# Keys and values given a place for the whole kernel, their rows fetched in the front's last steps, and edges counted in groups of two columns

## What is computed

```python
deg = maximum(segment_sum(ones, dst), 1)
h = relu(layernorm(x))
hw = norm * (h @ weight)                     # norm = deg ** -0.5
x = x + relu(segment_sum(hw[src], dst) * norm + bias)
x1 = relu(layernorm(x)); y = x1
for l in range(2):
    q, k, v = y @ Wq.T + bq, y @ Wk.T, y @ Wv.T
    scores = einsum(q[dst], k[src]) / 8      # softmax over the edges of one dst
    attn = segment_sum(softmax(scores) * v[src], dst) @ Wo.T + bo
    y = batchnorm(y + attn); y = batchnorm(y + ff(y))
x = x + layernorm(y)
```

## Time and profile before

| | |
|---|---|
| median of three runs | 3460.18 us |
| the profiled execution, its own time | 3465.55 us |
| its span, first to last instruction | 3463.7 us |
| PE, DVE, ACT, POOL busy | 3034.8, 2354.1, 1951.4, 2176.8 us |
| granted TensorE clock, mean | 0.960 |
| front's second part, first to last tile started | 359.5 to 936.8 us |
| attention of layer 0 begins | 991.2 us |

### The profile page before, as it was taken

How to read it: one execution, slowest core, us unless ns; L and a number is a source line. 1 busy time by engine, 2 the same in 40 slices (tenths; PEclk the granted TensorE clock), 3 DMA queues, 4 the chain that set the end, 5 groups by cost and what they waited for, 6 DMA issues and landing times. The chain is left out here.

```text
span 3463.7 us, 72225 instructions
## 1 busy us (share of the span) xinstructions
PE 3034.8 (88%) x24802; PEld 2390.4 (69%) x24802; DVE 2354.1 (68%) x6951; ACT 1951.4 (56%) x3918; POOL 2176.8 (63%) x1979
## 2 busy tenths in 40 slices
PE   2360899999947999999999989989999999999985
PEld 2120466666636888888888877767888888888875
DVE  9798344343426888888888854218888888888856
ACT  0120444444426777787877731227777787777734
POOL 2788888888006777777777720007777777777734
PEclk9995999999978999999999999999999999999987
DMA  9544776666379999998999841239999999999951
GB/s 371 81 82 94 148 133 118 125 121 123 97 171 167 166 166 166 175 167 166 168 165 168 154 98 24 48 73 171 165 165 166 169 173 165 164 164 171 153 121 59
DMA packets 1294527, 497.26 MB, mean 144 GB/s; under 512 B 1236806, under 2 KB 1262431, under 8 KB 1285974
## 3 DMA queue, kind: packets, MB, share of 16 engines
q1 hardware_dynamic: 1153262, 460.73, 67.5%
q0 software_dynamic: 133120, 0.80, 4.1%
q10 hardware_dynamic: 7788, 31.21, 2.7%
HBM read 154.06 MB, written 80.99 MB: 68 GB/s over the span
## 5 line engine op out<-in xcount | busy, mean ns | idle before, releaser
L1377 DVE CUSTOM_DVE_ANT_0 prob<-s_ps,mask 125x500 f32<-125x500 f32 x1600 | 1058.3, 673 | 307.6 <-PE s_ps L1224 231.1
L1146 POOL TENSOR_TENSOR staged<-prob,staged 125x500 f16<-125x500 f32 x960 | 1064.5, 1115 | 155.1 <-ACT staged L1140 85.8
L1314 ACT ACTIVATE prob<-prob,neg_max 125x1000 f32<-125x1000 f32 (+1 forms) x960 | 954.7, 994 | 120.7 <-DVE scrap L1383 118.3
L1224 PE MATMUL s_ps<-keys,queries 128*125 128x500 f16 x3200 | 947.2, 378 | 43.0 <-DMA values<-v_heads 25.4
L444 POOL DMA_INDIRECT counts<-count,cell x320 | 678.6, 2121 | 182.9 <-issue 106.8
L1255 PEld LDWEIGHTS o_ps<-values,across 125*125 125x125 f16 x7680 | 592.4, 139 | 223.1 <-issue 49.9
L1255 PE MATMUL o_ps<-values,across 125*125 125x128 f16 x7680 | 608.0, 222 | 60.6 <-DMA across<-staged 60.1
L1140 POOL CAST staged<-prob 125x500 f16<-125x500 f32 x640 | 385.5, 602 | 419.4 <-ACT prob L1314 259.1
L1390 DVE TENSOR_TENSOR p_lo<-t_ps,p_hi 125x500 f16<-125x500 f32 x640 | 431.6, 674 | 95.7 <-ACT p_hi L1324 95.0
L1235 PE MATMUL t_ps<-identity,prob 125*125 125x125 f32 x2560 | 413.2, 284 | 3.5 <-ACT agg L1334 2.9
L1324 ACT CAST p_hi<-t_ps 125x500 f16<-125x500 f32 x640 | 361.1, 564 | 87.4 <-PE t_ps L1235 87.0
(11 more groups left out here) (153 smaller groups left out, 3544.2 us busy)
## 6 DMA issues: line engine op xcount, KB each, us to landing
mask<-bias_rows SPq DMA_DIRECT2D x200, 218.8 KB
counts<-xt ACTq DMA_DIRECT2D x8, 3054.0 KB, 37.3
parts<-counts SPq DMA_DIRECT2D x20, 1093.8 KB
bias_rows<-edge_bias SPq DMA_DIRECT2D x20, 1093.8 KB
queries<-q_tiles SPq DMA_DIRECT2D x80, 250.0 KB, 3.9
pair_row<-pair_flat SPq DMA_DIRECT2D x40, 437.5 KB
across<-staged SPq DMA_TRANSPOSE x960, 3.3
q_tiles<-q_both SPq DMA_DIRECT2D x80, 125.0 KB, 3.1
```

What stands on the lines that cost most here:

```text
L1146: engine.tensor_tensor(here[0:P, BPC:2 * BPC, 0:P], prob[u % PROBS][:, k * KC:(k + 1) * KC].rearrange("p (s c) -> p s c", s=BPC), here[0:P ...
L1224: mm = pe.matmul(s_ps[n % SB][:, 0:KC], lhsT=queries[b][:, h, part, :], rhs=keys[:, h, c * KC:(c + 1) * KC], start=(part == 0), stop=(part ...
L1314: act.activation(here, here, ACT.Exp, bias=neg_max[u % 4][:, :], accum_out=sums[u // H % 2][:, u % H, piece:piece + 1]).then_inc(exped, 1)
L1377: dve.tensor_tensor_reduce(out=prob[u % PROBS][:, at], in0=s_ps[n % SB][:, 0:KC], in1=bias[b][:, at], scale=1.0, scalar=MASKED, op0=ALU.ad ...
```

## The change

1. A group is two columns (`GC` = 2, 160 groups of 250 edges), a batch four groups, so still 8 columns and 40 batches.
2. `keys` and `values` are allocated at the top, for the whole kernel. `hw` lies in the room of `values`, `parts` and `cnt` in that of `keys`; `w0_sb`, the one-hot tiles and `below` also lie in `keys`.
3. SP's loop: the stores come first in a step, the load of x next, the wait for the tile's groups and the load of `parts(t)` last, `parts` in two halves.
4. The keys and values of tiles 0 to 17 are read back from DRAM in steps 20 and 21; those of tiles 18 and 19 are copied from tile to tile in SBUF. The block waits for these copies, and PE waits for the read-back at the start of attention.
5. At the start of attention, in both layers, SP loads queries and mask of tile 0 alone; those of tile 1 and `wo` follow between the transposes of tile 0.

```diff
-GC = 4
+GC = 2
-PER_ROW = 2
+PER_ROW = 4
...
+        hw = values[:, :, :, :].rearrange("p h t e -> p (h t e)").bitcast(F32).rearrange("p (t d) -> p t d", t=NT)
+        parts = [keys[0:P, 2 * b:2 * b + 2, :].rearrange("p h n -> p (h n)").bitcast(U16) for b in range(2)]
+        cnt = [keys[0:P, 4 + 2 * b:6 + 2 * b, :].rearrange("p h n -> p (h n)").bitcast(F32) for b in range(2)]
...
+                def keys_back(heads):
+                    for h in heads:
+                        sp.dma_start(keys[:, h, 0:STAGED * P], k_heads[h * 128:(h + 1) * 128, 0:STAGED * P]).then_inc(keys_early, 16)
+
+                def values_back():
+                    for half in range(2):
+                        heads = slice(half * H // 2, (half + 1) * H // 2)
+                        load_rows(sp, values[:, heads, 0:STAGED, :].rearrange("p h t e -> p h (t e)"),
+                                  v_heads.rearrange("(h p) e -> p h e", h=H)[:, heads, 0:STAGED * 2 * DH], values_early)
+
+                def keys_straight(t):
+                    nodes = slice(t * P, (t + 1) * P)
+                    sp.wait_ge(k_low, t + 1)
+                    for part, tile in ((0, k_hi[t % 2]), (1, k_lo[t % 2])):
+                        for odd in range(2):
+                            sp.dma_start(keys[64 * part:64 * part + 64, odd::2, nodes],
+                                         tile[64 * odd:64 * odd + 64, :, :]).then_inc(keys_late, 16)
...
                 for t in range(NT + 3):
+                    if 0 <= t - 2 < NT:
+                        store_bias(t - 2)
+                    if t == NT + 1:
+
+                        keys_back(range(H // 2, H))
+                    if t >= 3:
+                        store_q(t - 3)
+                    if 3 <= t < NT + 1:
+                        store_k(t - 3)
+                    if t >= NT + 1:
+                        keys_straight(t - 3)
+                    if t == NT + 1:
+                        sp.wait_ge(cnt_t_used, NKC * NT)
+                        values_back()
+                    if 0 <= t - 2 < NT:
+                        store_x1(t - 2)
+                    if 3 <= t < NT + 1:
+                        store_v(t - 3)
+                    if t >= NT + 1:
+                        values_straight(t - 3)
+                    if t == NT:
+                        for b in range(2):
+                            sp.wait_ge(qkv_stored[b], QKV * STAGED // 2)
+                        sp.wait_ge(merged, NKC * NT)
+                        keys_back(range(H // 2))
...
                     if t < NT:
                         last_group = sp.value_load(needed_i[0:1, t:t + 1], min_val=1, max_val=NG)
                         sp.wait_ge(groups_landed, last_group)
                         if t >= 2:
                             sp.wait_ge(merged, NKC * (t - 1))
-                        load_rows(sp, parts[t % 2][:, :], counts_rows[t * P:(t + 1) * P, :], parts_loaded[t % 2])
...
+                        for side in range(SIDES):
+                            at = slice(side * N, (side + 1) * N)
+                            load_rows(sp, parts[t % 2][:, at], counts_rows[t * P:(t + 1) * P, at], parts_loaded[t % 2])
...
                 for c in range(NKC):
-                    if layer == 0 and c < 2:
-                        load_head(c)
                     load_mask(0, c)
-                if layer == 0:
-                    for h in range(2, H):
-                        load_head(h)
-                load_queries(1)
-                for c in range(NKC):
-                    load_mask(1, c)
-                sp.dma_start(wo_sb[:, :, :].rearrange("p c d -> p (c d)"), g["wo"][layer * 128:(layer + 1) * 128, :]
-                             ).then_inc(wo_loaded, 16)
...
-                    if layer == 0 and u < H and c == 0:
-                        pe.wait_ge(heads_loaded[h // 2], 2 * (16 + BOTH))
+                    if layer == 0 and u == 0 and c == 0:
+                        pe.wait_ge(g["keys_early"], H * 16)
```

More of the change, by code:

```diff
@@ L247, in front @@
         with ExitStack() as second:
-            parts = [sb(second, f"parts{b}", [P, ROW], U16) for b in range(2)]
-            cnt = [sb(second, f"cnt{b}", [P, N]) for b in range(2)]
             bias = [sb(second, f"edge_bias{b}", [P, N]) for b in range(2)]
@@ L1071, in attention @@
         wo_loaded = sem("wo_loaded")
-        heads_loaded = [sem(f"heads_loaded{h}") for h in range(H // 2)]
         q_loaded = [sem("q_loaded0"), sem("q_loaded1")]
@@ L1239, in weigh @@
                 def weigh(u, k):
+                    if layer == 0 and u == 0 and k == 0:
+                        pe.wait_ge(g["values_early"], 2 * BOTH)
                     if k == 0:
```

63 lines of the change are left out of this document (34 added, 29 removed).

## The result

The changed kernel takes 3419.73 us (median of four runs, 3414.44 to 3420.51), the kernel before on the same chip 3459.49 (four runs): a ratio of 0.9887, 95% interval 0.9872 to 0.9901. It gains 39.8 us, 1.1%, where 70.5 were forecast. The direction was right, and the time lies 6 us above the range's upper end.

The account below looks back on a forecast made before the run. The bounds attacked were PE's waits for DVE's tallies and for the DMA queue at attention's start. Gains of 43.3 and 27.2 us, 70.5, took 3465.55 to 3395, less 5.4 above the median: 3390 us, range 3362 to 3414.

Parts of the forecast that it names:

- POOL's last column: End of POOL's scatters in the front: from 868 before, four terms put it at 883.1 us, setting the last tile's start.
- The start of attention: Layer 0's five maxima, 79.1 us before, priced by layer 1's 35.8: 43.3 us gained.
- The read-back at the front's end: After the last tile's mask, one queue carries 9.9 MB at 240 GB/s, 41.3 us; front ends 71.2 behind the start.
- Rival 1: Nothing held back: groups land as in quiet, POOL ends at 862.5, time 3369, with a quick queue 3356; chance 0.22.
- The tallies: DVE's tallies ahead of the tiles: 280 ns less each at 250 elements, 78 us in all, ending at 262.
- price of a column: POOL in the front: 28 columns get the lower price once tallies end earlier, -5.5 us.
- stalls beside the early loads: POOL stops sooner while x and `w0` load, at most 9.2 us lost; half taken, 4.6.
- stalls in the burst of weights: POOL stops sooner in the burst of weights and `parts` behind `first_done`: 8.0 us taken, at most 9.2.
- stalls in the tile phase: POOL's waits for landings in each tile's burst of stores: 0 to 74 us, taken as 0.5 a tile, 8.
- Moving the stores ahead of the wait costs nothing: SP's loop: stores are of tiles 2 and 3 back, ready by then; a tile's 30 us cover `parts(t)`, which needs 6.
- Rival 2: More given back by bursts, tile phase, layer 0's start or a slower queue: singly 3398 to 3408, together over 3420; chance 0.18.
- Rival 3: POOL becomes the bound throughout: 3519 us, chance 0.03 slower; with 4.5 us in every tile's burst 3462, chance 0.02 unchanged.

Follow-up runs that it names:

- experiment 10: Changed kernel with queries 1, mask 1 and `wo` again ahead of the transposes at attention's start: 3412.25 us, ratio 0.9840 to the kernel before.
- experiment 11: The changed kernel run again unaltered, on one chip with its combined variant: 3420.53 us, ratio 0.9876 to the kernel before.
- experiment 12: Changed kernel with groups of four columns placed at the bursts and the old order at attention's start: 3393.16 us, ratio 0.9801 to the kernel before.
- experiment 9: Changed kernel with keys and values of tiles 0 to 17 read back at attention's start, not in the front's last steps: 3434.2 us, ratio 0.9919.
- experiment 3: Changed kernel with SP's wait for groups and the loads of `parts` back at the head of a step, stores behind: 3432.2 us, ratio 0.9917.
- experiment 5: Changed kernel loading only side 0 of the counts from tile 2 on, 0.6 MB less per burst: 3394.9 us, ratio 0.9818 to the kernel before.
- experiment 7: Changed kernel with groups of two in columns 0 to 223 and of four from 224 on: 3410.0 us, ratio 0.9837 to the kernel before.
- experiment 8: Changed kernel with groups of four in columns 0 to 39, 72 to 111 and 264 to 319, two elsewhere: 3397.65 us, ratio 0.9819.
- experiment 1: Changed kernel with groups of four columns again, all else kept: 3433.6 us, ratio 0.9914 to the kernel before.
- experiment 4: Changed kernel with groups of one column, eight groups to a batch: 3559.9 us, ratio 1.0277 to the kernel before.
- experiment 2: Kernel before with groups of two columns and nothing else changed: 3473.7 us, ratio 1.0043 to the kernel before.
- experiment 6: Changed kernel with four lanes instead of two sides, lanes 2 and 3 adding into spare cells: 3878.1 us, ratio 1.1162 to the kernel before.

## Why the prediction was half right

Step by step, in its order, by the changed kernel's profile:

| step | forecast | measured |
|---|---|---|
| a tally | 454 ns | 476 ns |
| tallies end; weights issued | 262; 267 | 268.9; 272.2 |
| first turns | 286 | 292.1 |
| POOL's last column | 883.1 | 910.0 |
| from there to the last turns | 9.7 | 9.9 |
| from the last turns to attention | 71.2 | 67.9 |
| from attention's start to the fifth maximum | 35.8 | 36.1 |
| span | 3393.2 | 3418.6 |

**The start of attention, right.** Layer 0 priced by layer 1: forecast 35.8 us, measured 36.1. The old order there, put back, changes nothing in the start's length (experiment 10), as the prediction had it; whether the new order costs some us later is open (experiments 11 and 12). From attention's start to the end of the kernel 41.7 us were gained, of 43.3 forecast.

**The read-back at the front's end, right.** 9.9 MB at 240 GB/s were forecast. The DMA view of 946 to 988 us of the changed kernel:

```profile
DMA packets 7265, 9.97 MB, mean 237 GB/s; under 512 B 5502, under 2 KB 5502, under 8 KB 7139
```

The tail came out 3.3 us shorter. Alone, though, the early fetch is worth 17 us (experiment 9), the difference between what it saves at the start and what it costs here; the prediction's two terms for it, 43.3 and -17.3, make 26, which still has the mask's order in it. Rival 1's quick queue, and its claim that nothing is held back, both fell.

**The tallies, right within 22 ns.** They end 7 us later than forecast. That it cost nothing at the end is argued: POOL waited for a batch's addresses only once in this stretch, 1.3 us, and PE was not the bound in the last tiles.

**The failed step: POOL's last column, 27 us late; with the tail's 3.3 us the other way it makes 24 of the 25.4 us that the span missed by.** The time missed by 29.7: the rest is mainly the 5.4 us that the forecast took off because the profiled execution before stood that much above its median; that of the changed kernel stands 0.6 above. Of the last column's terms, against 868 before:

| term | forecast | measured |
|---|---|---|
| price of a column | -5.5 | -21.1 |
| stalls beside the early loads | +4.6 | +6.0 |
| stalls in the burst of weights | +8.0 | +10.4 |
| stalls in the tile phase | +8 | +45.2 |

Small stalls beside the tallies add another 1.1 us. Of the stalls in the burst of weights 7.9 us are those ahead of column 77, inside a group, which the prediction's term, a wait between groups, did not hold.

- *"Most groups see quiet, so I take 0.5 a tile: 8."* This sentence failed. Its ends were 0 and 74 and I took a value near the lower one. The windows above give 46.6 us against 1.4. Some 2 us a tile came already while PE set the pace (27.6 us in 415, which is 13.4 tiles of 30.9): four times the 0.5.
- The other 19 us are a mechanism that the prediction lacked. It treated the bursts as given, each 30 us apart with their old size and place, and nothing in it let a late POOL make POOL later. But once POOL is the bound, SP stands at the wait when the last group lands, and `parts` and the held-back stores go out as one burst, right onto the scatters of the next tile. *"Moving the stores ahead of the wait costs nothing"*, with the 30 us of a tile as cover, looked at the stores' own readers only. In fact the order gains 7 to 18 us in the front (experiment 3), and still the stores of step t+1 stand behind the wait of step t: `parts` and they make the burst in which the 5 us stalls fall. That the stall shrinks with the burst is shown by experiment 5, that it needs the small groups by experiments 7 and 8, in which POOL is the bound at the end, the groups are wide and the stalls are gone. What the stores alone cost was not tried.
- *"28 columns get the lower price: -5.5"* missed in the kind direction. A column's issue took 2055 ns, in the mean of all 320, against 2121 before, 21 us in all, and 19.5 of these lie in the first 100 columns. With groups of four it is back at 2126 (experiment 1), with one at 2020 (experiment 4): beside narrower tallies an issue on POOL is cheaper. I had counted the shorter time beside tallies and not that each tally also disturbs less.
- Rival 2 was the right story (the bursts cost 9.2 each and the tile phase 20), with its largest term again below what was measured. Rival 3's unchanged case, 4.5 us in every tile's burst, is close to what the groups of two do in the kernel before (experiment 2: last column 937.7, where it had 955), and its slower case to the groups of one (experiment 4).

**What a landing costs.** Landings in quiet, with the packets gone 1.8 us behind the issue, would have put the last column at 862.5; it came at 910.0, since landings in a burst are longer: behind 127 us POOL idled up to 6.67 us ahead of a group, with two more columns issued since. The Trainium skill, DMA: Bandwidth & Descriptors, "Anatomy of one DMA", has a fixed 2.0 us a DMA; the landings in quiet fit that figure and those in a burst do not. The Trainium skill, DMA: Bandwidth & Descriptors, "Latency and other measured facts", says that the latency to HBM, of which most of the fixed cost consists, rises under load to 2 us; the long ones of these stalls, 4.75 to 6.67 us, are two to three times that.

## What to carry to other kernels

Where a loop runs on small groups, each waiting for the landing of the one before last, price the smaller group not by the landing in quiet alone but also by the landing in the worst burst, times the number of bursts, and take the spread between both as the range. Ask what an in-order queue that waits for a late producer will issue the moment the wait ends: if the answer is a load and all stores held back behind it, the producer's next steps will be hit by it, and lateness grows. A size that helps one engine and hurts another need not be the same everywhere: wide groups where the bursts are and narrow ones elsewhere gained 22 us over narrow ones throughout (experiment 8 against the changed kernel, by medians on different chips).

## What the runs showed of the hardware that was not expected

- The landing of an indirect DMA that adds depends on where it writes: sent over and over to the same 500 cells, columns left stalls of 17.39 and 24.45 us, 571 us in all, in a kernel that otherwise has 84, and other queues suffered too: the DMA engines were busy for 1.00 of a stretch at 31 GB/s, instead of 0.59 at 122 (experiment 6). Why is open.
- The issue of an indirect DMA on POOL is cheaper the narrower the instructions are that DVE runs beside it. From 127.8 to 240 us, the mean of one issue by the timeline is 2291, 2071 and 2012 ns beside tallies of 500, 250 and 125 elements (the kernel before, the changed one, experiment 4); between 400 and 700 us, where there are no tallies, it is 2069 ns before and 2073 in the changed kernel. In experiment 4 it is 2022 there, so the width is not all of it.
- A PE that waits tile by tile pays for each wait a little more than its length. The first eight of the last tile's turns took 2.04 us after 8.41 us of idle, at a granted clock of 0.50 (the lower level, 1.2 GHz), like the first eight of all (2.01); after no idle they took 1.03. From 300 to 715 us, where PE hardly waits, the granted clock is 1.00, from 715 to 919.9, where it is idle for 41 of 205 us, 0.89. Within the whole second part PE was busy 11 us longer than before for the same work, at a clock of 0.96 instead of 1.00.

```profile
919.86 2.04 PE L843 MATMUL turn_ps<-identity,keys 125*125 125x125 f32 x8 [8.41 <-DVE keys L656]
```
